# Dealing VectorE's work out in smaller portions beside the matmuls of an adapter-and-mixing kernel

## What is computed

```python
c = einsum('bsi,boi->bso', x, weight[adapter_ids])            # 512x2048 by 2048x2048, per batch
c_norm = c * rsqrt(mean(c * c, -1) + eps)
H_res, H_pre, H_post = logits(c_norm @ W.T)                   # 16 + 4 + 4 numbers per token
H_res = sinkhorn_log(H_res, num_iters=50, tau=0.1)            # 4x4 per token, rows and columns in turn
H_res = (1 - g) * I + g * H_res
y = einsum('btnc,btn->btc', streams(c), softmax(H_pre)) @ W_branch
out = x + einsum('btij,btjc->btic', H_res, streams(c)) + einsum('btc,btn->btnc', y, softmax(H_post))
```

## Time and profile before

| | us |
|---|---|
| median of 3 runs | 1854.85 (1852.56 to 1856.22) |
| the profiled execution, its own time | 1854.1 |
| its span, first to last instruction | 1852.0 |
| PE busy | 1698.9 (92% of the span) |
| DVE busy | 1578.4 (85%) |
| ACT busy | 648.4 (35%) |
| POOL busy | 47.2 (3%) |

### The profile page before, as it was taken

The page is one execution under the profiler, slowest core; times in us unless marked ns, Lnnn a source line. Parts: engine busy times, 40 slices in busy tenths (PEclk is TensorE's granted clock), DMA queues, the critical chain, the costliest instruction groups (busy, mean ns, idle before and its releaser), DMA issues.

```text
span 1852.0 us, 24465 instructions
## 1 busy us (share of the span) xinstructions
PE 1698.9 (92%) x7690; PEld 1366.3 (74%) x7690; DVE 1578.4 (85%) x6128; ACT 648.4 (35%) x1031; POOL 47.2 (3%) x40
## 2 busy tenths in 40 slices
PE   9999999989999999899999989999999999999704
PEld 7888887777877788787877778777887778777601
DVE  4323599996999889996999969998799978999899
ACT  4334433333233433234333433234332343332503
POOL 0000000000000000000000000000000000000404
PEclk9999999999999999999999999999999999999857
DMA  6224323453335523263234532355233633336002
GB/s 232 91 90 140 123 92 114 151 196 109 97 110 193 181 92 126 92 229 123 92 122 135 198 125 92 114 175 193 87 117 100 227 129 99 116 117 216 9 1 91
DMA packets 65073, 237.72 MB, mean 128 GB/s; under 512 B 7344, under 2 KB 7472, under 8 KB 64816
## 3 DMA queue, kind: packets, MB, share of 16 engines
q1 hardware_dynamic: 64944, 236.17, 38.2%
HBM read 202.58 MB, written 33.55 MB: 128 GB/s over the span
## 4 chain that ended last, share of the span: by engine, by line
DVE 65%; PE 28%; issue 2%; DMA 2%; ACT 2%; SPq 1%; DVEq 0%; ACTq 0%
PE acc L976 25%; DVE piece L851 16%; DVE w_lo L612 10%; DVE work L788 9%; DVE vec L786 8%; DVE vec L784 8%; DVE xpre L817 3%; DVE cond_t L650 3%; DVE x_lo L620 2%; DVE x_raw L877 2%; DMA w_raw<-wt 1%; DVE xpre_t L828 1%; SPq L218 1%; DMA out<-piece 1%; DVE xpre L815 1%
## 5 line engine op out<-in xcount | busy, mean ns | idle before, releaser
L976 PE MATMUL acc<-w_hi,x_hi 128*128 128x512 f32 x2048 | 817.2, 399 | 2.1 <-DVE w_lo L612 2.1
L976 PE MATMUL acc<-w_hi,x_lo 128*128 128x512 f32 x2048 | 803.9, 393 | 0.0
L976 PE MATMUL acc<-w_lo,x_hi 128*128 128x512 f32 x2048 | 803.0, 392 | 0.0
L976 PEld LDWEIGHTS acc<-w_hi,x_hi 128*128 128x128 f32 x2048 | 388.8, 190 | 83.8 <-DVE w_lo L612 2.4
L976 PEld LDWEIGHTS acc<-w_hi,x_lo 128*128 128x128 f32 x2048 | 387.7, 189 | 83.7
L976 PEld LDWEIGHTS acc<-w_lo,x_hi 128*128 128x128 f32 x2048 | 388.7, 190 | 78.0
L612 DVE TENSOR_TENSOR w_lo<-w_raw,w_hi 128x1024 fp32r<-128x1024 f32 x256 | 312.2, 1222 | 157.1 <-ACT w_hi L382 153.7
L382 ACT ACTIVATE w_hi<-w_raw 128x1024 fp32r<-128x1024 f32 x256 | 270.0, 1057 | 450.8 <-DMA w_raw<-wt 450.6
L851 DVE SCALAR_TENSOR_TENSOR piece<-cond,kern,piece 128x512 f32<-128x512 f32 x448 | 301.5, 745 | 0.0
L788 DVE TENSOR_TENSOR work<-kern,vec 128x32 f32<-128x32 f32 x1536 | 251.1, 202 | 0.0
L786 DVE RECIPROCAL vec<-vec 128x8 f32<-128x8 f32 x1536 | 242.3, 199 | 0.1
(11 more groups left out here) (109 smaller groups left out, 747.8 us busy)
## 6 DMA issues: line engine op xcount, KB each, us to landing
w_raw<-wt SPq DMA_DIRECT2D x256, 512.0 KB, 3.5
x_raw<-xt SPq DMA_DIRECT2D x64, 512.0 KB, 4.5
piece<-xn SPq DMA_DIRECT2D x56, 512.0 KB, 4.4
out<-piece SPq DMA_DIRECT2D x56, 512.0 KB, 3.4
x_raw<-xn SPq DMA_DIRECT2D x8, 512.0 KB, 4.6
out<-x_raw SPq DMA_DIRECT2D x8, 512.0 KB, 2.7
cond<-wb SPq DMA_DIRECT2D x1, 1024.0 KB, 14.6
cond<-wall SPq DMA_DIRECT2D x1, 192.0 KB, 12.6
```

Source lines behind the costliest of these rows:

```text
L976: mm = nc.tensor.matmul(acc[t][:], stationary, moving, start=(chunk == 0 and m == 0), stop=(chunk == CHUNKS - 1 and m == 2))
```

## The change

All of it concerns the order in which VectorE's work stands, and the places of other engines that belong to it.

- The scaling is dealt out in single pairs (`PAIRS_AT`: between 8 and 23 pairs in each of 16 units), not in whole rounds of six pairs; the waits in which both halves were joined at the end of each portion are left out. Each half now waits only for its own last step (`chain`), also across units.
- The four instructions of `pre` become `pre_term` and alternate with pairs, or with steps of the mix in unit 24.
- The mix is cut into 40 steps (`mix_term`: one stream or y, added to two outputs, two instructions), 2 to 4 in a unit. One step is moved to unit 1 and four are moved to unit 2 of the next batch (33 and 34 in `MIX_AT`); in the last batch all of them stay within it (`MIX_AT_LAST`).
- `pre` of tiles 1 and 2 moves by one unit (12 to 13, 16 to 17), with their turning and splitting; the branch product of tile 1 moves from unit 17 to 18, the turning of tile 3 from 26 to 27, its splitting from 27 to 28.
- SyncE stores each piece in the unit after its last step, so the last two of a batch in units 0 and 3 of the next, and the x load no longer waits for stores.
- The number of instructions that compute or move data is the same.

```diff
-FAST_AT = ((5, 12), (13, 20))
-FINAL_AT = 20
-PRE_AT = (8, 12, 16, 24)
-PRE_T_AT = (10, 14, 23, 26)
-PRE_SPLIT_AT = (11, 15, 24, 27)
-Y_AT = (13, 17, 25, 28)
-MIX_AT = (21, 22, 24, 25, 26, 27, 29, 30)
+PAIRS_AT = {4: 20, 5: 20, 6: 20, 7: 20, 8: 10, 9: 17, 10: 20, 11: 17,
+            13: 10, 14: 19, 15: 23, 16: 20, 17: 8, 18: 23, 19: 19, 20: 22}
+FINAL_AT = 21
+PRE_AT = (8, 13, 17, 24)
+PRE_T_AT = (10, 15, 23, 27)
+PRE_SPLIT_AT = (11, 16, 24, 28)
+Y_AT = (13, 18, 25, 28)
+MIX_TERMS = STREAMS + 1
+MIX_AT = {21: 3, 22: 4, 23: 4, 24: 2, 25: 4, 26: 3, 27: 3, 28: 3, 29: 3, 30: 3, 31: 3, 33: 1, 34: 4}
...
+def mix_plan(last):
+
+    terms, plan = 0, {}
+    for U, count in (MIX_AT_LAST if last else MIX_AT).items():
+        plan[U] = [divmod(k, MIX_TERMS) for k in range(terms, terms + count)]
+        terms += count
+    return plan
...
-                if pieces_of is not None:
-
-                    for slot in range(OUT_SLOTS):
-                        sp.wait_ge(stored[slot], count)
...
-                        if end and U == STORE_AT[q]:
...
+                        if b > 1 and stores_at(False)[q] + 1 == U + UNITS:
+                            store(b - 2, q)
+                        if end and stores_at(last)[q] + 1 == U:
+                            store(b - 1, q)
...
+                def scale_pairs(number):
+
+                    for _ in range(number):
+                        if pairs[0] % PAIRS == 0:
+                            chain[:] = count[0], count[0]
+                        side, part = divmod(pairs[0] % 6, 3)
...
+                        for h in range(2):
...
+                            after(chain[h])
...
+                            chain[h] = mark(ins)
...
-                    for q in range(MIX_PAIRS):
-                        if U == MIX_AT[q]:
-                            mix(q // 2, q % 2)
-                    for t in range(TILES):
-                        if U == PRE_AT[t]:
-                            pre(t)
...
+                    steps = mix_plan(last).get(U, ())
+                    for place, (q, j) in enumerate(steps):
+                        if U in PRE_AT and place < STREAMS:
+                            pre_term(PRE_AT.index(U), place)
+                        mix_term(c, 1 - parity, q, j)
...
+                    if b > 1:
+                        for q, j in mix_plan(False).get(U + UNITS, ()):
+                            mix_term(c - 1, parity, q, j)
```

More of the change, by code:

```diff
@@ L251, in ending @@
             def ending():
+                store(BATCHES - 2, MIX_PAIRS - 1)
                 load_last_residual(MIX_PAIRS - 1)
@@ L271, in rows, with store @@
                 return t[bass.ds(place, 1), :, :].rearrange("a p (s c) -> (a p) s c", s=2)
+            def store(c, q):
+                sp.wait_ge(mixed, 1 + c * MIX_PAIRS + q + 1)
+                sp.dma_start(rows(out, c * MIX_PAIRS + q), piece[:, q % OUT_SLOTS, :, :]
+                             ).then_inc(stored[q % OUT_SLOTS], 16)
             def body(b, parity, end):
@@ L607, in _ @@
         def _(dve):
+            term_written, count = [0, 0], [0]
             def w_low(b, unit):
@@ L667, in after @@
                 def after(number):
-                    dve.wait_ge(step, c * DVE_STEPS + number)
+                    dve.wait_ge(step, number)
                 def link(ins):
@@ L749, in log_step @@
                     else:
+                        after(chain[1])
                         ask(tt(vec[:, SUM, :], vec[:, B, :], vec[:, INV, :], ALU.mult))
@@ L770, in log_step @@
                     link(tt(work_r, work_r, over_columns(INV), ALU.mult))
[L772 to L791, removed]
@@ L804, in final_matrix, with pre_term @@
                         dve.wait_ge(matrix_ready, 1)
-                def pre(t):
-                    if t > 0:
+                weighed = [0]
+                def pre_term(t, j):
+                    if t > 0 and j == 0:
                         dve.wait_ge(pre_turned, c * TILES + t)
[L811 to L823, removed]
+                    weight = logit[:, t, NRES + j:NRES + j + 1]
+                    source = cond[:, 1 - parity, j, t, :]
+                    if j == 0:
+                        weighed[0] = mark(nc.vector.tensor_scalar(xpre[:], source, weight, None,
+                                                                  ALU.mult))
+                        return
+                    after(weighed[0])
+                    ins = nc.vector.scalar_tensor_tensor(
+                        out=xpre[:], in0=source, scalar=weight, in1=xpre[:],
+                        op0=ALU.mult, op1=ALU.add)
+                    if j < STREAMS - 1:
+                        weighed[0] = mark(ins)
+                    else:
+                        ins.then_inc(pre_ready, 1)
                 def pre_low(t):
@@ L830, in pre_low @@
                                             ).then_inc(pre_lo_ready, 1)
[L832 to L857, removed]
@@ new lines, in mix_term @@
+                def mix_term(c, side, q, j):
+                    (t, p), slot = divmod(q, 2), q % OUT_SLOTS
+                    if j == 0:
+                        dve.wait_ge(residual_in[slot], (c * 2 + q // OUT_SLOTS + 1) * 16)
+                    for s in range(2):
+                        i = 2 * p + s
+                        if j < STREAMS:
+                            source = cond[:, side, j, t, :]
+                            weight = kern[:, t * NRES + i * STREAMS + j:][:, 0:1]
+                        else:
+                            source = y_ps[t % 2][:]
+                            weight = logit[:, t, NRES + STREAMS + i:][:, 0:1]
+                            if s == 0:
+                                dve.wait_ge(y_ready, c * TILES + t + 1)
+                        if j > 0:
+                            after(term_written[s])
+                        ins = nc.vector.scalar_tensor_tensor(
+                            out=piece[:, slot, s, :], in0=source, scalar=weight,
+                            in1=piece[:, slot, s, :], op0=ALU.mult, op1=ALU.add)
+                        if j == STREAMS and s == 1:
+                            ins.then_inc(mixed, 1)
+                        else:
+                            term_written[s] = mark(ins)
```

56 lines of the change are left out of this document (33 added, 23 removed).

## The result

The changed kernel takes 1813.83 us (median of 4 runs, 1813.25 to 1814.47) against 1854.06 for the kernel before on the same chip (4 runs, 1852.56 to 1856.22): ratio 0.9782, 95% interval 0.9765 to 0.9799. It is 40 us faster. Forecast were 1808.5 us.

A forecast was written before the change was run, and what follows sets the result against it. PE paces, waiting only for DVE, 92 us over its floor in seven batches. With 6.5 us a batch left (45.5), 46 us go: 1854.1 becomes 1808, median 1808.5 us; forecast 1797 to 1820 (0.62), wider range 1788 to 1832.

The forecast's parts named there:

- The floor: An undisturbed batch takes 203.3 us of PE's own work; seven are 1423, against 1515.5 measured, so 92 us to win.
- Unit 20 pins the lag: `cond_t` can't start before 4.45 us in unit 20, so DVE begins list 21 3.8 late, whatever earlier lag below 3.3.
- The wait for `piece` grows to 4.4: In unit 23 mix 1 ends later, so PE's wait before turning tile 2 grows from 3.0 to 4.4 us, restart included.
- The waits for `cond_t` go: PE's waits of 1.79 and 0.76 in the second half and 3.33 at the next unit 0 disappear.
- Rival 1: The mix wait in unit 23 goes too: 1766 us; chance 0.14 together with the stretch below 1797.
- Rivals 2 to 4: DVE heavier than its prices, 1824 (0.16); VectorE becomes the bound, 1865 (0.05); no effect, border stall returns, 1851 to 1858 (0.03).
- their prices: DVE's time per operation from the old profile: `w_lo` 1.14 us, a pair 0.232, a mix step 1.33, `pre` alternating 2.4.
- finer interleaving: Pairs between long instructions: could cost under 0.232 us each, or 0.1 more for 12 pairs beside `pre`, giving 1813.5 us.
- the 6.5 us a batch: Time left over the floor in each of seven batches: 6.0 in units 23 and 24 plus 0.5 in unit 28.
- With the slower clock 6.0 a batch: Units 23 and 24: the 4.4 us wait for `piece` plus 1.6 of slow clock, taken from batch 5.
- 0.5 a batch: Unit 28: a new wait of PE, `pre_low` of tile 3 done at 6.9, branch product wants it at 6.35.
- five steps, 6.6 us, left those lists, and the store wait is gone: Units 29 to 31: argument against rival 4, that DVE's lag grows again there and the border stall returns.

The follow-up runs named there:

- turn_later: The changed kernel with the turning and branch product of tile 2, and pre and branch product of tile 3, one unit later, mix steps rearranged: 1772.95 us.
- experiments 1 and 3: 1 is turn_later; 3 is turn_later with 14 pairs also moved from unit 20 to units 18 and 19: 1763.4 us.
- no_carry: The changed kernel with all 40 mix steps of every batch within the batch, none carried into the next: 1817.54 us.
- experiment 7: The turn_later kernel with 14 pairs moved from unit 20 to 18 and 19, and no mix steps carried into the next batch: 1801.25 us.
- mix1_in_22: The changed kernel with three mix steps moved from list 23 to list 22, so mix 1 ends ahead of list 23's `w_lo`: 1799.74 us.

## Why the prediction was right, and by how much it was off

**The floor** (203.3 us): shown by the version that runs at it. **Unit 20 pins the lag**: shown by the row of `cond_t` at 4.45 and by two runs that changed the lag ahead of it, to 5.4 and to 0.3; in the first, list 21 gained only the idle time ahead of the pin. **The wait for `piece` grows to 4.4** (idle 4.2): it did, 4.21. **The waits for `cond_t` go**: all did; they had been 48.1 / 7 = 6.9 us a batch in the mean, and not the 8 of batch 5 that the prediction gives for every batch. Rival 1 (1766) stayed away for the reason given there; it takes turn_later to bring its time about. Rivals 2 to 4 fell: DVE's lists come out slightly under their prices (list 20 begins 2.1 us late, forecast 2.8). List 8 of batch 5, a `pre` dealt between pairs, takes 5.64 us where they give 5.84, so that finer interleaving gains a little and does not cost.

**Off was the size of two terms** of the 6.5 us a batch. The profiled execution is 5.2 us over its forecast of 1808, and 5.9 over what the sum gives before rounding (92.2 - 45.5 = 46.7 less, 1807.4).
- "With the slower clock 6.0 a batch" for units 23 and 24 was 6.45: undisturbed they take 12.26 by the prediction (12.17 in experiments 1 and 3), now 18.7 in the mean. The clock loss was taken over from one batch with 2.9 us of idle time (1.6); what comes on top of the idle time was forecast as 1.8, restart included, and is 2.25 in the mean. Seven batches: 3.1 us.
- "0.5 a batch" in unit 28 was 1.1 in six batches and nothing in the seventh, 6.5 us in place of 3.5: 3.0 more. The sum left out the restart (0.2 to 0.3) and a wait of DVE's for `x_hi` that stands right behind the pin:

```profile
1226.44 0.69 DVE L670 TENSOR_TENSOR cond_t<-turn_ps,cond_t 128x512 fp32r<-128x512 f32 x1 [2.30 <-ACT cond_t L535]
1227.38 1.22 DVE L640 TENSOR_TENSOR x_lo<-x_raw,x_hi 128x1024 fp32r<-128x1024 f32 x1 [0.26 <-ACT x_hi L407]
1228.53 0.68 DVE L853 TENSOR_TENSOR xpre_t<-y_ps,xpre_t 128x512 fp32r<-128x512 f32 x1
```

Together 6.1, of 5.7 that the batches are over the forecast (1474.7 - 1423.5 = 51.2 against 45.5).

**Wrong was a reason, not a number**: the prediction set "five steps, 6.6 us, left those lists, and the store wait is gone" against the stall's return at the border. The border, measured as above and in the mean of the six, took 20.5 us in the kernel before, 18.8 there without the store wait, 15.3 in no_carry and 14.3 in the changed kernel: 10 us of the 37 are the store wait, 6 the carry (the whole run shows 4), and 21 are neither. Those 21 can be read from DVE's time from the start of list 24 to the start of the next batch's list 0, in batch 5 before and then in no_carry (columns of the earlier trace rows):

```profile
1221.26:1283.22 61.96, 60.48 (x273) 48.90 (x272) 61.85 (x86) 23.75 (x33) 0.00 (x0) 0.98 0.59 202
1198.55:1259.67 61.12, 60.38 (x269) 48.72 (x269) 60.45 (x83) 23.54 (x33) 0.00 (x0) 0.97 0.64 221
```

Before, DVE was busy throughout these lists, and PE took 54.5 us for its eight units, so that the lag grew from 0.2 to 7.6. In no_carry it grows to 5.2, and the wait at the border falls from 3.3 to 1.0. Two things make the difference. The lists hold one mix step less and a `pre` that is dealt out: 1.4 us less work. And PE takes 56.3 us, 1.7 more: 1.1 for the wait in unit 28 and 0.6 for slow clock in unit 24; some of that passes as idle time of DVE. So a part of it is no gain of the order: PE loses time there, and DVE catches up. Once PE loses none, and list 24 begins 2.4 late instead of 0.4, the border's wait without the carry is back, at up to 4.7 us (experiment 7). The joins have no part in it, as these lists hold no pairs. This division is worked out from the traces; no run takes the parts one by one in the kernel before.

## What to carry to other kernels

- Where an engine's list holds an instruction that can't start before a fixed point of the other engine's work, an engine that gets there early waits, and its lead from before is lost: work belongs ahead of that instruction, as much as the idle time before it holds, and what stands behind it is late for the next consumer.
- When one order is changed, look for the last piece of work on which the next consumer waits, and count its distance from such a point. Here moving the consumer by one unit, and the branch product behind it, gave as much again (41 us) as the whole change.
- An edit's worth depends on the idle time around it: the same five steps were worth 4 us beside a stall and 38 without it. Price an edit in the version in which it is to live.

## What the runs showed of the hardware

TensorE's clock after a wait. Before, the same idle time of 2.85 to 2.88 us ahead of the turning was followed by a granted clock of 1.00 in three batches (the first of the two windows of before above), by a mean of 0.90 in three and of 0.81 in one. After 3.1 us (mix1_in_22) it stayed at 1.00 in two batches and fell in five; after 4.2 us it fell in all seven. Three windows of 1 us in batch 5, behind the turning at 1192.43:

```profile
1193.00:1194.00 1.00, 1.00 (x5) 0.90 (x4) 1.00 (x2) 0.45 (x1) 0.00 (x0) 0.50 0.87 348
...
1197.00:1198.00 1.00, 1.00 (x3) 0.72 (x3) 1.00 (x3) 0.00 (x0) 0.00 (x0) 0.50 0.00 0
1198.00:1199.00 1.00, 1.00 (x6) 0.81 (x5) 1.00 (x3) 0.00 (x0) 0.00 (x0) 0.97 0.00 0
```

The clock is at 0.50, 1.2 of 2.4 GHz, until about 1198, with PE busy throughout; the 28 matmuls of unit 24 take 8.2 us. In the seven batches, restart and slow clock together cost 1.35 to 2.9 us beyond the idle time. What decides between the seven wasn't found. Waits of 1.0 to 1.3 us (turn_later, no_carry) showed no such loss.
